# Unscaled attention maps, biases added on GpSimd, gate products as stages, and new order lists in a small vision tower with experts

## The chip, the cores and the metric

The kernel runs on one core of one Trainium2 chip, in float32 (a few counting matrices are bfloat16). The time is the device time of one execution in microseconds; the kernel before takes 390.56 us, the median of 3 runs (388.23 to 392.81).

## The reference

The input is 32 images of 3x96x96. Every image becomes 36 tokens of 128 features (1152 tokens in all), which pass through four blocks, each on the layer-normed sum so far, and each added to it. `norm` is a layer norm. Cut to what matters here:

```
h = tokens(x)                                  # patches, projection, norm
# block 1: attention with rotary positions, then a relu network; both normed behind the addition
src = norm(h)
x1 = norm(src + softmax(rope(q) rope(k)^T * hd**-0.5) v @ Wo.T, g1, be1)
h = h + norm(x1 + relu(x1 @ W1.T + b1) @ W2.T + b2, g2, be2)
# block 2: two lower-triangular products over the features
h = h + gelu(norm(h) @ tril(W1).T + b1) @ tril(W2).T + b2
# block 3: differential attention, then a group norm of the context
o = (softmax(q1 k1^T / sqrt(hd)) - lam * softmax(q2 k2^T / sqrt(hd))) v
h = h + (groupnorm(o) * gn_w + gn_b) @ out_w.T + out_b
# block 4: attention, then 64 experts, 2 for each token
x = norm(h); x = x + softmax(q k^T * hd**-0.5) v @ wo
x2 = norm(x); gates, ids = top_2(softmax(x2 @ wr))
y = gelu(x2[slots] @ w1[e] + b1[e]) @ w2[e] + b2[e]
h = h + x + sum over 2 of gate * y
```

There are 8 heads of 16 features, and an expert takes up to 72 tokens.

## The kernel before, in words

The tokens are worked on in four blocks of 8 images (288 tokens, `b` from 0 to 3). The way through the network is cut into stages, and a stage with its block is written `rope_scores:2`. The prefixes name the part: `tok` and `src` are the token stage and the first norm, `rope` is the attention of block 1, `x1`, `net` and `x2` its norm, network and second norm, `mix` block 2, `dif` and `gn` block 3, `moe` the attention of block 4, `rt` the routing. The endings name the work:

- `_norm_a`: VectorE takes the mean and variance (L1203, L1206), then GpSimd makes the reciprocal root in four small instructions (L611 to L615; more of them for `moe`). `_norm_b`: ScalarE applies it. `x2_norm_b` goes on: GpSimd multiplies and adds two rows (L663, L664), and VectorE adds it to `h` (L1327).
- `_turn`: TensorE transposes, and ScalarE copies back. `_qk`, `_v`: projections.
- `_scores`: TensorE makes the scores of all heads and pairs of images in four PSUM banks (`scores`), VectorE takes the row maximum (L1266) and subtracts it (L1275) into `ex`, ScalarE takes the exponential in place. A map is 100 partitions x 1152.
- `_sums`: VectorE sums the rows (L1284), takes the reciprocal (L1291) and multiplies the map by it (L1299) into `probs`. For `dif` the two maps are scaled in place, and `dif_mix` subtracts them (L1309) into `probs`.
- `_flip`: TensorE transposes the map in four parts (L803), ScalarE copies each into `pT`. `_pv`: TensorE multiplies by the values, and ScalarE copies the context to `ctxT`. `_out`: the output projection, which VectorE adds to the running sum (L1318).
- `mix_out` and `dif_out` open their bank with `biased`, a product of a row of ones and the bias row, so that the bias is in the sum.
- `gn_sum`, `gn_center`, `gn_var`, `gn_rstd`, `gn_apply`: the group norm. At its end VectorE multiplies by the scale, ScalarE adds `gn_b`, and only then `dif_out` can start.
- `rt_logits`, `rt_gate`, `rt_count`: VectorE finds the two best experts and their gates, TensorE counts the places, VectorE makes the slot numbers `flat_u`, and GpSimd sends the rows to their slots in DRAM with six indirect DMAs a block (L690). VectorE also makes `gm`, the gates as a matrix of tokens by experts, from which the bias of the experts' second layer comes.

What order the work has is written out by hand: `ORDERS_FOUND` has a list of stages for each of TensorE ("pe"), ScalarE ("act"), VectorE ("dve") and GpSimd ("pool"), and each engine works through its list strictly in order, waiting on semaphores. PSUM has four banks besides `scores`, and the jobs of TensorE go over them in rotation: `fill` waits until the reader of four jobs before is done. `AWAKE_FOUND` gives the number of filler products (`wT` by `wT`, 128x128) that TensorE does ahead of a stage, into the bank that the stage will use. A float32 product is two instructions in the trace, a transposition one.

Behind the lists, TensorE turns `gm`, multiplies by `b2` (`bias_turn`, `bias`), and VectorE copies (`bias_in`) and adds it to `h` (`bias_add`). Then for each of the six DMAs of the last block TensorE waits for its landing (`last_sent`) and does `PACE` fillers, then `HEAD_WARM` more. SyncE waits for the same landings and loads the rows of the experts in nine chunks of 2 to 8 experts (L570). TensorE transposes an expert's rows (L979), VectorE scales them (L1408), and the 64 experts run, one behind the other: 4 products of the first layer, gelu on ScalarE, 4 products of the second layer, VectorE scales by the gates (L1437), GpSimd scatters (L720). The weights come through a ring of 11. At the end the results are loaded, summed and stored.

What the change touches in the code: the lists and constants at the top, `taken`, `tokens`, `biased`, `flip`, `weigh`, the branches of `mix_out` and `dif_out`, `bias_turn` and `bias` on TensorE; `_scores` and `gn_apply` on ScalarE; `_scores`, `_sums`, `_out` and `bias_in` on VectorE.

## Time and profile before

| what | value |
| --- | --- |
| median of 3 runs | 390.56 us (388.23 to 392.81) |
| the profiled execution | 389.98 us |
| its span in the profile | 388.3 us |
| mean granted clock of TensorE | 0.959 |
| TensorE busy | 347.7 us (90%) |
| VectorE busy | 233.7 us (60%) |
| ScalarE busy | 220.9 us (57%) |
| GpSimd busy | 197.4 us (51%) |

The profile is of one execution. PE is TensorE, PEld its weight loads, DVE VectorE, ACT ScalarE, POOL GpSimd, SPq the queue of SyncE. Busy time is the time in which an engine had an instruction under way; TensorE's fillers count in it. The mean duration of TensorE's small products is longer than the time each adds, since they overlap. The granted clock is a share of 2.4 GHz: 1.00 is the upper level and 0.50 the lower (1.2 GHz). "Idle before" an instruction is given with what ended it.

### The profile page before, as it was taken

To read this page: it belongs to the slowest core of one execution; us is meant where nothing else is said; L and a number is where in the kernel's file an instruction comes from. 1 tells how busy PE (TensorE), PEld (TensorE's weight loads), DVE (VectorE), ACT (ScalarE), POOL (GpSimd) and SP (SyncE) were. 2 spreads that over 40 slices of the span, in tenths; PEclk is the share of its full clock that TensorE was granted. 3 is DMA by queue.
4 is the path that set the end of the run, shared out by engine and by line. 5 is a ranking of instruction groups with operands and counts; after the bars stand their busy time and mean duration, and the time that the engine had idled before them with its cause. 6 is when DMAs were issued, how large, how long until landed. Compare 5 with 4: busy or idle time off the path is not lost.

```text
span 388.3 us, 11371 instructions
## 1 busy us (share of the span) xinstructions
PE 347.7 (90%) x4424; PEld 315.2 (81%) x4424; DVE 233.7 (60%) x615; ACT 220.9 (57%) x640; POOL 197.4 (51%) x312
## 2 busy tenths in 40 slices
PE   8969799999988999997899899499999999999950
PEld 8748687887866889696778788399999999999950
DVE  1446788763489899897868985623335433333314
ACT  1247677777659876677488563103555555555520
POOL 3169687587841112236345767720555555555550
PEclk9999999999999999998999999559999999999995
DMA  7999924000000000000000100037899989999206
GB/s 277 374 391 334 150 28 125 2 2 1 2 3 0 3 3 2 3 2 3 3 3 2 33 9 13 15 95 202 272 320 316 322 308 316 327 324 314 85 9 182
DMA packets 21239, 50.20 MB, mean 129 GB/s; under 512 B 4116, under 2 KB 10340, under 8 KB 21058
## 3 DMA queue, kind: packets, MB, share of 16 engines
q1 hardware_dynamic: 18146, 46.96, 37.9%
q0 software_dynamic: 3040, 2.52, 2.4%
q8 instruction: 36, 0.59, 0.6%
q14 instruction: 17, 0.14, 0.1%
HBM read 43.97 MB, written 7.72 MB: 133 GB/s over the span
## 4 chain that ended last, share of the span: by engine, by line
PE 57%; DVE 12%; ACT 11%; POOL 9%; DMA 6%; issue 4%; SPq 1%; POOLq 0%; DVEq 0%
PE bank L728 34%; PE scores L728 18%; DMA lambdas<-in_lambdas 4%; ACT work L1037 4%; PE bank L803 3%; ACT norm L1037 3%; POOL rstd L613 3%; DVE mx L1266 2%; DVE stats L1203 2%; DVE work L1275 1%; ACT src L1037 1%; PE bank L979 1%; POOL rstd L611 1%; ACT xrow L1037 1%; POOL norm L664 1%
## 5 line engine op out<-in xcount | busy, mean ns | idle before, releaser
L1037 ACT ACTIVATE work<-scores,b1T 128x72 f32<-128x72 f32 x256 | 61.3, 322 | 66.9 <-PE scores L728 66.9
L728 PE MATMUL bank<-ring,work 128*72 128x128 f32 x512 | 97.3, 274 | 0.0
L720 POOL DMA_INDIRECT expert_rows<-work,put_u x64 | 59.9, 935 | 61.7 <-issue 37.7
L728 PE MATMUL scores<-work,ring 128*128 128x72 f32 x512 | 89.0, 258 | 0.2 <-ACT work L1037 0.2
L728 PEld LDWEIGHTS scores<-work,ring 128*128 128x128 f32 x512 | 76.9, 191 | 0.3 <-issue 0.3
L728 PE MATMUL bank<-wT 128*128 128x128 f32 x504 | 72.3, 283 | 2.7 <-ACT work L1037 2.7
L728 PEld LDWEIGHTS bank<-wT 128*128 128x128 f32 x504 | 63.8, 193 | 5.7 <-ACT work L1037 3.1
L1037 ACT ACTIVATE work<-bank 128x288 f32<-128x288 f32 (+3 forms) x136 | 46.7, 376 | 34.4 <-PE bank L728 27.0
L1437 DVE TENSOR_SCALAR work<-bank,work 72x128 f32<-72x128 f32 x64 | 22.2, 347 | 67.5 <-PE bank L728 67.5
L728 PEld LDWEIGHTS bank<-ring,work 128*72 128x72 f32 x512 | 53.8, 145 | 0.2 <-ACT work L1037 0.2
L611 POOL TENSOR_SCALAR rstd<-mv 96x3 f32<-96x3 f32 x32 | 10.1, 315 | 54.8 <-DVE mv L1206 53.6
L613 POOL TENSOR_TENSOR rstd<-rstd,minus_half 96x3 f32<-96x3 f32 x32 | 28.2, 882 | 2.7
L690 POOL DMA_INDIRECT slot_rows<-xrow,flat_u x24 | 24.0, 1001 | 10.5 <-issue 6.1
L1408 DVE TENSOR_SCALAR work<-bank,cols 128x72 f32<-128x72 f32 x64 | 21.7, 341 | 6.8 <-PE bank L979 6.8
L728 PE MATMUL bank<-xTp,wT 128*128 128x288 f32 x80 | 22.9, 416 | 2.3 <-ACT work L1037 1.4
L1037 ACT ACTIVATE work<-work 100x1152 f32<-100x1152 f32 (+1 forms) x20 | 20.2, 1016 | 8.3 <-DVE work L1275 7.0
L1266 DVE TENSOR_REDUCE mx<-scores 100x32 f32<-100x1152 f32 x16 | 21.6, 1351 | 5.0 <-PE scores L728 4.9
L728 PE MATMUL bank<-wT,xTp 128*128 128x128 f32 x192 | 23.8, 277 | 0.4 <-DVE work L1252 0.4
L728 PEld LDWEIGHTS bank<-wT,xTp 128*128 128x128 f32 x192 | 22.5, 192 | 1.4 <-issue 1.2
L1284 DVE TENSOR_REDUCE sm<-work 100x32 f32<-100x1152 f32 x16 | 21.4, 1340 | 3.5 <-ACT work L1037 3.3
L1299 DVE TENSOR_TENSOR work<-work,sm 100x1152 f32<-100x1152 f32 x16 | 21.8, 1360 | 0.6
L1275 DVE TENSOR_TENSOR work<-scores,mx 100x1152 f32<-100x1152 f32 x16 | 21.7, 1358 | 0.6
(159 smaller groups left out, 594.2 us busy)
## 6 DMA issues: line engine op xcount, KB each, us to landing
ring<-in_experts SPq DMA_DIRECT2D x64, 512.0 KB, 5.0
work<-in_patches SPq DMA_DIRECT2D x3, 864.0 KB, 10.6
slot_rows<-hid SPq DMA_DIRECT2D x1, 2340.0 KB, 30.2
work<-slot_rows SPq DMA_DIRECT2D x7, 292.5 KB
wT<-in_weights SPq DMA_DIRECT2D x1, 1664.0 KB, 13.9
expert_rows<-mid POOLq DMA_DIRECT2D x2, 576.0 KB, 5.1
ring<-expert_rows SPq DMA_DIRECT2D x4, 288.0 KB, 4.0
expert_rows<-work,put_u POOLq DMA_INDIRECT x64, 4.4
```

Source lines behind the costliest of these rows:

```text
L611: st.step(pool.tensor_scalar(n, m, -1.0, None, ALU.mult))
L613: st.link(pool.tensor_tensor(r, r, minus_half[0:TP, 0:TPB], ALU.pow))
L690: pool.indirect_dma_start(out=xslot[:, :], out_offset=bass.IndirectOffsetOnAxis(ap=flat_u[:, TPB * b + n, k:k + 1], axis=0), in_=xrow[:, b ...
L720: pool.indirect_dma_start(out=ytok[:, :], out_offset=bass.IndirectOffsetOnAxis(ap=put_u[:, e:e + 1], axis=0), in_=ys[0:CAP, e % NY, :], in ...
L728: return nc.tensor.matmul(o, a, b, start=start, stop=stop)
L1037: return nc.scalar.activation(o, i, f, **kw)
L1266: st.link(v.tensor_reduce(m3, sc, AX_X, ALU.max))
L1275: v.tensor_tensor(e4, sc, m3.unsqueeze(3).broadcast_to([SROWS, QUADS, 2 * PAIRS, SEQ]), ALU.subtract).then_inc(S["exp_in"], 1)
L1284: st.link(v.tensor_reduce(s3, e4, AX_X, ALU.add))
L1299: v.tensor_tensor(to, e4, s3.unsqueeze(3).broadcast_to([SROWS, QUADS, 2 * PAIRS, SEQ]), ALU.mult).then_inc(S["map_scaled" if stage[:3] == ...
L1408: v.tensor_scalar(xe[:, e % NX, :], banks[i][:, 0:CAP], col("L1_ffn_ln2_g"), col("L1_ffn_ln2_b"), ALU.mult, ALU.add).then_inc(S["xe_ready" ...
L1437: v.tensor_scalar(ys[0:CAP, f % NY, :], banks[f % 2][0:CAP, 0:D], xrows[0:CAP, f, D + 1:D + 2], None, ALU.mult).then_inc(S["ys_ready"], 1)
```

## The change

- In `rope` and `moe` the exponentials go from ScalarE straight to `probs`, unscaled, and `_flip` waits for the exponential alone. `_sums` only sums and takes the reciprocal, into `part_of_one`. A new stage `_flat` (TensorE, ScalarE) multiplies `part_of_one` by the identity, in four small products, so that the reciprocals lie as 8 heads by 288 tokens (`flat`). `_pv` has a second job: `spread` (which repeats a head's value over its 16 features) by `flat`. VectorE then multiplies `ctxT` by it (new stage in its list, L1362 of the new kernel), and `_out` waits for that.
- The bias rows of `mix_out` and `dif_out` are added by GpSimd (new stages `mix_norm_b`, `dif_norm_b`, L721 and the like of the new kernel, 96x384 each, 8 in all) into `mid`, and `_out` adds the product to `mid`; `biased` is gone. ScalarE's part of `gn_apply` is gone: `gn_b` is multiplied by the output weights once (new stage `fold`) and added to the row of `out_b`.
- `bias_turn`, `bias` and `bias_in` become stages `gate_turn` and `gate_bias` in the lists, with the copy on ScalarE and other banks.
- `HEAD_WARM` goes from 4 to 10, `PACE` from 3 to 4, and all the lists are new. The fillers of `AWAKE_FOUND` are 270 instead of 252; by part: tok 26 (16 before), src 10 (6), rope 12 (24), x1 3 (2), net 1 (4), mix 32 (38), dif 70 (64), gn 20 (14), moe 43 (39), rt 53 (45).

```diff
-HEAD_WARM = 4
-PACE = 3
+HEAD_WARM = 10
+PACE = 4
...
-    tok_z:0=5 tok_shift:0=4 tok_shift:1=1 tok_turn:1=2 tok_z:3=1 tok_turn:2=1 src_turn:0=3 rope_qk:0=4 tok_turn:3=2
+    tok_z:0=12 tok_shift:0=3 tok_shift:1=2 tok_z:2=2 tok_shift:2=2 tok_turn:2=4 src_turn:0=1 tok_turn:3=1
...
+                if stage == "mix_norm_b":
+
+                    pool.tensor_tensor(tiles(mid, b), tiles(h, b), row("L0_ffn_b2"), ALU.add).then_inc(S["mix_based"], 1)
+                if stage == "dif_norm_b":
+
+                    pool.wait_ge(S["folded"], 1)
+                    pool.tensor_tensor(tiles(mid, b), tiles(h, b), row("L1_attn_out_b"), ALU.add).then_inc(S["dif_based"], 1)
...
-            def biased(job, name):
-
-                o = fill(pe, job)
-                pe.wait_ge(S["rows_in"], 16)
-                mm(o[0:TP, 0:TPB * D], const("ones")[0:1, :], rows[0:1, ROWS.index(name), :].unsqueeze(1).broadcast_to([1, TPB, D]),
-                   start=True, stop=False)
...
-                    pe.wait_ge(S["probs_ready"], probs_count[name + "_sums", b])
+                    pe.wait_ge(S["exp_done"], soft_n[name + "_scores", b] + 1)
...
+                if name == "dif":
+                    return
+                job = (stage, b, 1)
+                o = fill(pe, job)
+                pe.wait_ge(S["flat_ready"], flat_count[name + "_flat", b])
+                mm(o[:, 0:TB], const("spread", H), flat[:, n % 2, :]).then_inc(filled(job), 1)
+
+            def flatten(stage, b):
+
+                job = (stage, b, 0)
+                o = fill(pe, job)
+                name = stage.split("_")[0]
+                pe.wait_ge(S["sums_ready"], soft_n[name + "_scores", b] + 1)
+                tokens_of = const("ident")[0:SROWS, :].rearrange("r (a k) -> r a k", k=HALF)[:, :, 0:SEQ]
+                for p in range(PAIRS):
+                    last = mm(o[0:H, 2 * SEQ * p:2 * SEQ * (p + 1)], part_of_one[:, flip_n[name + str(b)] % 2, p, :], tokens_of)
+                last.then_inc(filled(job), 1)
...
                 elif stage == "dif_out":
-                    biased((stage, b, 0), "L1_attn_out_b")
-                    pe.wait_ge(S["square_ready"], square_n["gn_apply", b])
-                    tokens((stage, b, 0), ctx_tile, [block_of("L1_attn_out_w")], open_=True)
+                    pe.wait_ge(S["gn_scaled"], b + 1)
+                    tokens((stage, b, 0), ctx_tile, [block_of("L1_attn_out_w")])
...
-            bias_turn(0)
-            bias_turn(1)
-            bias(0, banks[0])
-            bias_turn(2)
-            bias(1, banks[1])
-            bias_turn(3)
-            bias(2, scores[:, 2, :])
-            bias(3, scores[:, 3, :])
+            pe.wait_ge(S["gmT_ready"], NB)
...
+                elif stage in ("rope_pv", "moe_pv"):
+                    dve.wait_ge(S["ctx_ready"], ctx_count[stage, b])
+                    r = read(dve, (stage, b, 1))
+                    v.tensor_tensor(ctxT[:, tok], ctxT[:, tok], r[:, 0:TB], ALU.mult).then_inc(S["ctx_scaled"], 1)
...
-                    base = {"rope": src, "net": mid, "mix": h, "dif": h, "moe": src}[name]
+                    base = {"rope": src, "net": mid, "mix": mid, "dif": mid, "moe": src}[name]
+                    if stage in ("mix_out", "dif_out"):
+                        dve.wait_ge(S["mix_based" if stage == "mix_out" else "dif_based"], b + 1)
```

How the instructions now stand, at three places. The names are those of the tiles: `scores`, `bank` and `ex` (within `work`) as above, `sm` the row sums, `cst` the constants. First VectorE at the first attention map, before:

```order
L1266 TENSOR_REDUCE mx<-scores 100x32
L1275 TENSOR_TENSOR work<-scores,mx 100x1152
L1252 TENSOR_TENSOR work<-bank,cst 128x288 x4
L1284 TENSOR_REDUCE sm<-work 100x32
L1291 RECIPROCAL sm<-sm 100x32
L1299 TENSOR_TENSOR work<-work,sm 100x32x36
L1266 TENSOR_REDUCE mx<-scores 100x32
L1275 TENSOR_TENSOR work<-scores,mx 100x1152
```

And VectorE at the same place in the new kernel:

```order
L1298 TENSOR_TENSOR work<-bank,cst 128x288 x4
L1312 TENSOR_REDUCE mx<-scores 100x32
L1321 TENSOR_TENSOR work<-scores,mx 100x1152
L1386 TENSOR_TENSOR rows<-rows,bank 96x128
L1334 TENSOR_REDUCE sm<-work 100x32
L1335 RECIPROCAL part_of_one<-sm 100x4x4x2
L1312 TENSOR_REDUCE mx<-scores 100x32
L1321 TENSOR_TENSOR work<-scores,mx 100x1152
L1362 TENSOR_TENSOR work<-work,bank 128x288
```

The rotary products of the next block (x4) now stand ahead of the first map, the scaling of the map is gone, and a fold and the multiplication of the context have come in.

Second GpSimd between the first attention and the second norm, from `x1_affine:2` on, before:

```order
L714 TENSOR_TENSOR mid<-norm,rows 96x384
L715 TENSOR_TENSOR mid<-mid,rows 96x384
L611 TENSOR_SCALAR rstd<-mv 96x3
L612 TENSOR_SCALAR rstd<-mv 96x3
L613 TENSOR_TENSOR rstd<-rstd,minus_half 96x3
L615 TENSOR_TENSOR rstd<-rstd 96x3
```

And the same place in the new kernel:

```order
L733 TENSOR_TENSOR mid<-norm,rows 96x384
L734 TENSOR_TENSOR mid<-mid,rows 96x384
L721 TENSOR_TENSOR mid<-h,rows 96x384
L623 TENSOR_SCALAR rstd<-mv 96x3
L624 TENSOR_SCALAR rstd<-mv 96x3
L625 TENSOR_TENSOR rstd<-rstd,minus_half 96x3
L627 TENSOR_TENSOR rstd<-rstd 96x3
```

The new addition of a bias row, `mix_norm_b:0`, stands ahead of two reciprocal roots (one of them is listed).

Third TensorE at the end of the lists, from the last logits on, before (`wr` are the logits, `run` the last count, `wT` alone fillers, `gm` the gate turns and `b2nat` the gate products):

```order
L728 MATMUL bank<-wr,xT 96x64 x3
...
L728 MATMUL bank<-run,ones 96x64
L964 MATMUL scores<-cst,gm 64x96 x6
L728 MATMUL bank<-b2nat,work 96x128 x3
L964 MATMUL scores<-cst,gm 64x96 x3
L728 MATMUL bank<-b2nat,work 96x128 x3
L964 MATMUL scores<-cst,gm 64x96 x3
L728 MATMUL scores<-b2nat,work 96x128 x6
L728 MATMUL scores<-wT 128x128 x22
L979 MATMUL bank<-cst,work 128x72 x3
```

And in the new kernel:

```order
L747 MATMUL bank<-wr,xT 96x64 x3
L985 MATMUL scores<-cst,gm 64x96 x3
L747 MATMUL scores<-b2nat,work 96x128 x6
L747 MATMUL bank<-wT 128x128 x6
...
L747 MATMUL bank<-run,ones 96x64
L985 MATMUL scores<-cst,gm 64x96 x3
L747 MATMUL bank<-b2nat,work 96x128 x6
L747 MATMUL scores<-wT 128x128 x34
L1019 MATMUL bank<-cst,work 128x72 x3
```

Two of the four gate products and six fillers have moved ahead of the last count, only one gate turn and two products are left behind it, and 34 fillers stand where 22 stood.

## Rows read from the trace of the kernel before

**Rows 1.** Stretches: length, then busy us and instructions; PEclk, DMA share, GB/s.

```profile
38.20:85.10 46.90, 43.11 (x731) 37.51 (x730) 36.24 (x75) 33.72 (x86) 33.94 (x53) 1.00 0.40 65
85.10:110.10 25.00, 23.38 (x160) 19.04 (x158) 12.27 (x48) 16.95 (x40) 18.51 (x33) 1.00 0.00 1
110.10:187.00 76.90, 70.72 (x1277) 61.49 (x1277) 69.84 (x116) 56.08 (x127) 22.57 (x45) 0.98 0.01 2
187.00:235.50 48.50, 44.60 (x777) 39.63 (x776) 39.82 (x120) 33.52 (x87) 27.78 (x51) 1.00 0.04 11
235.50:248.40 12.90, 8.16 (x75) 7.23 (x73) 8.71 (x36) 4.08 (x8) 9.03 (x16) 0.83 0.05 13
248.40:256.70 8.30, 7.58 (x33) 6.03 (x33) 1.93 (x5) 0.00 (x0) 5.62 (x6) 0.50 0.05 12
256.70:264.60 7.90, 7.42 (x48) 7.22 (x47) 2.49 (x6) 0.00 (x0) 0.00 (x0) 0.73 0.65 173
264.60:374.40 109.80, 109.52 (x1086) 108.93 (x1086) 40.92 (x139) 61.33 (x256) 57.71 (x62) 1.00 0.80 271
```

**Rows 2.** Groups by line and form: busy us, mean ns of one, idle before.

```profile
L1284 DVE TENSOR_REDUCE sm<-work 100x32 f32<-100x1152 f32 x16 | 21.4, 1340 | 3.5 <-ACT work L1037 3.3
L1291 DVE RECIPROCAL sm<-sm 100x32 f32<-100x32 f32 x12 | 4.2, 353 | 0.4
L1299 DVE TENSOR_TENSOR work<-work,sm 100x1152 f32<-100x1152 f32 x16 | 21.8, 1360 | 0.6
L1252 DVE TENSOR_TENSOR work<-bank,cst 128x288 f32<-128x288 f32 x16 | 6.2, 448 | 0.0
L979 PE MATMUL bank<-cst,work 72*128 72x72 f32 x64 | 14.4, 228 | 0.5 <-DVE work L1408 0.5
L728 PE MATMUL bank<-xTp,wT 128*128 128x288 f32 x80 | 22.9, 416 | 2.3 <-ACT work L1037 1.4 <-DVE h L1318 0.9
L728 PE MATMUL bank<-rows,cst 1*96 1x384 f32 x16 | 7.0, 520 | 0.0
L1037 ACT ACTIVATE work<-work,cols 128x288 f32<-128x288 f32 x4 | 2.1, 526 | 0.0
```

**Rows 3.** Timeline (start, us), VectorE and GpSimd: an addition alone, and pairs that meet.

```profile
79.93 0.55 DVE L1327 TENSOR_TENSOR h<-h,norm 96x384 f32<-96x384 f32 x1 [0.28 <-POOL norm L664]
94.00 1.27 DVE L1327 TENSOR_TENSOR h<-h,norm 96x384 f32<-96x384 f32 x1 [2.81 <-POOL norm L664]
93.86 1.00 POOL L714 TENSOR_TENSOR mid<-norm,rows 96x384 f32<-96x384 f32 x1
54.27 1.36 DVE L1299 TENSOR_TENSOR work<-work,sm 100x1152 f32<-100x1152 f32 x1
54.30 1.37 POOL L615 TENSOR_TENSOR rstd<-rstd 96x3 f32<-96x3 f32 x1
```

**Rows 4.** Timeline of VectorE: the addition of the first attention's last block.

```profile
85.09 0.55 DVE L1318 TENSOR_TENSOR src<-bank,src 96x384 f32<-96x384 f32 x1 [1.72 <-PE bank L728]
```

**Rows 5.** Timeline: the last attention's last block on VectorE, and ten fillers on TensorE.

```profile
228.90 1.36 DVE L1299 TENSOR_TENSOR work<-work,sm 100x1152 f32<-100x1152 f32 x1
235.55 0.55 DVE L1318 TENSOR_TENSOR src<-bank,src 96x384 f32<-96x384 f32 x1 [0.92 <-PE bank L728]
224.56 2.48 PE L728 MATMUL bank<-wT 128*128 128x128 f32 x20
```

**Rows 6.** Timeline from the last scatters to the first expert, and GB/s of 256:266.

```profile
248.41 1.01 POOL L690 DMA_INDIRECT slot_rows<-xrow,flat_u  x1 [0.80 <-POOL xrow L681]
256.75 1.02 DVE L1399 TENSOR_TENSOR h<-bank,h 96x384 f32<-96x384 f32 x2 [2.20 <-DMA slot_rows<-xrow,flat_u]
256.79 7.16 PE L728 MATMUL scores<-wT 128*128 128x128 f32 x44
264.06 0.61 DVE L1408 TENSOR_SCALAR work<-bank,cols 128x72 f32<-128x72 f32 x2 [5.36 <-PE bank L979]
GB/s 65 7 0 0 0 0 4 83 254 83 87 262 287 316 241 229 200 200 200 200 166 200 200 200 200 200 200 200 200 200 200 200 200 200 200 200 200 200 200 200
```

261 lines of the change are left out of this document (150 added, 111 removed).

## The prediction

> **What bounds the kernel now.** I first cut the run into stretches [rows 1]. From 264.6 to 374.4 us TensorE is busy for 109.52 of 109.80 us at granted clock 1.00 (the upper of its two levels, 2.4 GHz): the 64 experts. The change leaves their instructions alone, so this stretch and the 13.9 us behind it only shift. Ahead of it stand 264.6 us. TensorE is busy there too, but with filler multiplications in part, which the list of fillers adds to keep its clock up, so its share says little. The engine to look at is VectorE: 36.24 of 46.90 us in the first attention, 12.27 of 25.00 in the stretch behind it, 69.84 of 76.90 in the differential one, 39.82 of 48.50 in the last one. So VectorE sets the pace in the attentions, nearly without gaps in the differential one. In 85.1 to 110.1 it idles for half the time: there GpSimd is busy for 18.51 of 25.00 us with reciprocal roots and affine steps.
>
> Then I read the groups of costs [rows 2]: each attention map costs VectorE a sum (1340 ns), a reciprocal (353) and a scaling multiplication (1360). Last I read the way from the last attention block to the first expert [rows 6]: the final scatter lands at about 256.75 (VectorE waited for it 2.20 us), TensorE starts 22 fillers (x44, two instructions each) at 256.79 and needs 7.16 us, and VectorE then reads the first turned expert input at 264.06. The nine loads of rows are issued from 256.8 on. In the window 256 to 266, cut in 40 parts of 0.25 us, traffic starts at 257.5. By 258.5 about 106 KB have moved (4, 83, 254 and 83 GB/s, times 0.25 us), and the first load has 73 KB. So the fillers, not the load, end this wait.
>
> **The first attention, 38.2 to 110.1.** The scaling goes: 4 x 1.36 = 5.44 us of VectorE. In its place comes a multiplication of the context, 128x288 with one operand in PSUM. Its nearest row is the 128x288 multiplication from PSUM at 448 ns [rows 2]: 4 x 0.45 = 1.8. The fold (96x128, once) has no row; it lies between a few tenths and the 0.55 us that the 96x384 addition takes [rows 5], I take 0.3. VectorE saves 5.44 - 1.8 - 0.3 = 3.3 us.
> The map may also be turned as soon as the exponential is there; sum, reciprocal and scaling (3.05 us) no longer stand ahead of it. At 85.09 VectorE had waited 1.72 us for the last block's product [rows 4]; of such waits I take back 1.5.
> Against it, GpSimd gets eight additions of 96x384 at 1.0 us ([rows 3], L714). One stands ahead of the x2 roots, where GpSimd is the engine waited for: +1.05. The second must be done before the mix_out:1 addition of VectorE, which stood right behind x2_norm_b:3; behind that wait in VectorE's queue are the norms and the first differential maximum: +0.45. TensorE gets, per attention block, 4 small products and one of 128x288. By the nearest rows (228 ns for one instruction of 72x72, 416 for one of 128x288, which overlap) that is at least 0.7 and at most 4 x 2 x 0.23 + 2 x 0.42 = 2.7 us; I take 1.0, since its instructions overlap like the 288-wide ones (22.9 us for 80). Fillers in the rope stages fall from 24 to 12, and at 0.248 us each (2.48 us for 10, [rows 5]) 3.0 us of them make room for 4.0. Net I book nothing there. If that cover is gone the cost is the product's whole 4 x 2.7 = 10.8 us less 3.0.
> Sum: -3.3 - 1.5 + 1.5 = -3.3 us. Ends: +4 (no wait returns, each extra step on the way) and -7.
> The start is booked at nothing: seven more fillers stand before tok_z:0 (1.7 us), but later patches were waited for anyway, and rope_qk:1 is only moved ahead of the first maximum.
>
> **The differential attention, 110.1 to 187.** VectorE's work stays. Gone are ScalarE's shift by gn_b (526 ns, four times, on the way to dif_out) and the bias products (7.0 us for 16 instructions, [rows 2]) from mix_out and dif_out. Since VectorE idles for only 7.06 us here, that is all there can be to win; I take 1. New are the other six or seven GpSimd additions, where GpSimd is busy for 22.57 of 76.90 us. They are free by occupancy, but they share something with VectorE [rows 3]: the same VectorE addition h+norm takes 0.55 us alone and 1.27 us when GpSimd's L714 has started 0.14 us before it, and GpSimd's little L615 takes 1.37 us instead of 0.19 when it starts 0.03 us behind VectorE's scaling. Each addition can hold up VectorE by 0 to 1.0 us. VectorE's operations with both operands in SBUF (8 scalings of 1.36 us, 4 differences of the same shape, 8 of 128x288 at about 0.45) fill some 20 of the 77 us, so roughly one addition in three meets one, for half its length: I take +1. Sum 0, ends -5 and +5.
>
> **The last attention and the routing, 187 to 256.7.** VectorE saves 4 x (1.36 - 0.45) = 3.6 us. Of the last block, 6.65 us passed from the start of the scaling (228.90) to the addition of its product (235.55) [rows 5]. Now, from the end of the reciprocal, VectorE does the routing of block 2 (about 3.1 us, as before), the context multiplication 0.45, then waits for the product, about 1.5: 5.1, so -1.5. Ahead of the last turn, logits and count stand eight more fillers net (2.0 us), mostly beside waits: +0.6. Behind it the chain is kept: roots, norm, count, six scatters of about 1.27 us from 248.41 on. Sum -4.5, ends -8 and 0.
>
> **The bias products and the wait for the first expert.** The gate turns and products become stages before the scatters land, and 24 of the 34 fillers are spread over the six waits for scatters. Behind the last one remain 4 + 10 = 14. At 0.248 us they take 3.5 us, where 7.16 stood; at half clock 14 x 0.43 = 6.0 (7.16 us for 22 already mixes both levels). The load has landed by then. The row of 248.4 to 256.7 shows 0.50 granted, though TensorE was busy for 7.58 of 8.30 us, so I take a little off the 3.7: -3.3, ends -1.1 and -4. If they lagged more, the load (2 us) would not be what is late next but the fillers again.
>
> **The sum.** -3.3 + 0 - 4.5 - 3.3 = -11.1 us against the profiled run's 389.98 us (span 388.3 and 1.68 around it): 378.9. The median of the runs is 390.56, 0.6 above the profiled one, so 379.5.
>
> **Rivals.**
> 1. GpSimd's queue takes the gain. For: its additions (8.4 us) and the excluded pairs above; and the first six scatters (7.6 us) stand ahead of rt_norm_a:2 in its queue, while VectorE's list now has the statistics of that step sooner behind them; in TensorE's queue the turn of that block stands ahead of the last map's turning. Price: the first attention's 3.3 us vanish and about 1.5 in the last: 384.3. Against: GpSimd idles for over two thirds of the differential stretch.
> 2. More comes back: VectorE's idle time in the differential and last attention (7.1 + 8.7 us) shrinks by a third, since the maps turn earlier and the banks come free sooner: -5, so 374.5. Against: those waits are for work that mostly stays.
> 3. Slower: TensorE's clock falls in the first attention. The place is 38.2 to 85.1, where it was at 1.00 with 43.11 of 46.90 us busy, and where half of the fillers go. Only the stretch behind 248.4 shows the lower level (0.50, 1.2 GHz), after one in which TensorE was busy for 8.16 of 12.90 us [rows 1]. At half clock some 38 us of real work (43.11 less about 5 of fillers) become 76. Over half of the stretch that adds some 15 us against the 11 gained: 395. It decides from about a third of the stretch at half clock. Against: 4 us of new products per attention fill the same places.
> 4. The lists keep their old waits and only the end gains: 390.6 - 3.3 = 387.3, with small costs 388.5.
>
> **How the numbers follow.** The forecast gets 0.50, rival 1 0.20, rival 2 0.16, rival 3 0.08, rival 4 0.06. A measurement here tells about 1% (3.9 us) from no change. Faster by more than that (under 386.7): forecast and rival 2 nearly whole, most of rival 1: 0.82. Within 1%: rival 4, the rest of rival 1 and little of rival 3: 0.10. Slower: 0.08. The range goes from 373 (rival 2) to 388 (rival 1 and part of rival 4).
>
> **What would show it.** Right: the scaling rows at half their count (8 of 16), eight context multiplications near 0.45 us; the differential stretch still about 77 us long with VectorE over 90% busy; 3 to 4 us from the last landed scatter to the first turned input plus 0.3; the expert stretch again 110 us. Wrong: TensorE's clock under 0.9 before the routing; VectorE's two-input rows well over 1.36 us; GpSimd as releaser of VectorE or ScalarE for longer in sum than before; an end wait that is still over 6 us.

## The result, and the profile after

The changed kernel takes **392.09 us** (389.04 to 394.71, 20 runs), the kernel before 390.65 us (388.23 to 393.46, 20 runs): a ratio of 1.0047, 95% interval [1.0028, 1.0067]. It is slower by half a per cent, within the 1% that I called no change. Forecast were 379.5 us and a range of 373 to 388. The profiled execution took 391.9 us, its span is 390.2.

To see where the forecast 11 us went I put the same events of the two traces side by side, start to start:

| event | before | after | difference | added in this part |
| --- | --- | --- | --- | --- |
| first map maximum | 38.24 | 40.52 | +2.3 | +2.3 |
| last context addition of the first attention | 85.09 | 94.49 | +9.4 | +7.1 |
| first differential maximum | 111.09 | 119.17 | +8.1 | -1.3 |
| first maximum of the last attention | 179.07 | 186.24 | +7.2 | -0.9 |
| last landed scatter | 256.75 | 260.80 | +4.1 | -3.1 |
| first scaled expert input | 264.06 | 265.74 | +1.7 | -2.4 |
| span | 388.3 | 390.2 | +1.9 | +0.2 |

From the differential attention on it goes much as forecast. All of the loss lies ahead of the last context addition at 94.49 us, so I looked there first. In the slices of the span (40 of 9.76 us each) the fifth and sixth stand out, TensorE's busy share in the one and its clock in the other (the last line is the clock of the kernel before, in its slices of 9.71 us):

```profile
PE   8999699999999899999999999799999999999950
...
PEclk9999969999999999999999999969999999999995
...
PEclk9999999999999999998999999559999999999995
```

The granted clock fell in the sixth slice, where the kernel before kept it at 8 or 9 up to the routing. The stretches of 2 us show what came ahead of that fall (columns as in [rows 1]):

```profile
46.00:48.00 2.00, 0.00 (x0) 0.00 (x0) 0.53 (x2) 0.45 (x2) 1.39 (x2) 0.99 1.21 163
48.00:50.00 2.00, 0.96 (x25) 0.77 (x26) 0.19 (x1) 0.00 (x0) 0.59 (x1) 0.50 0.88 110
50.00:52.00 2.00, 2.00 (x13) 2.00 (x13) 1.97 (x2) 0.57 (x2) 0.00 (x0) 0.50 0.20 36
52.00:54.00 2.00, 2.00 (x14) 1.78 (x13) 0.56 (x1) 1.07 (x3) 0.00 (x0) 0.50 0.00 0
54.00:56.00 2.00, 2.00 (x73) 1.57 (x70) 0.00 (x0) 1.01 (x3) 0.00 (x0) 0.81 0.00 0
```

TensorE did nothing at all in 46 to 48 us, and from 48 on its clock was at 0.50 (1.2 GHz) for about 7 us, of which it idled for the first one. The timeline of TensorE tells what it had been doing, the 64 products of one map:

```profile
44.42 0.69 PE L747 MATMUL scores<-work 32*36 32x72 f32 x40
49.04 0.71 PE L747 MATMUL scores<-work 32*36 32x72 f32 x24 [3.93 <-issue]
```

It stopped in the middle of `rope_scores:1`, and the wait has no releaser: "issue" means that nothing the profile shows was waited for. No semaphore stands between those products. The trace of before has the same stop, half as long, and its clock stayed at 1.00:

```profile
44.45 0.78 PE L728 MATMUL scores<-work 32*36 32x72 f32 x52
47.05 0.35 PE L728 MATMUL scores<-work 32*36 32x72 f32 x12 [1.82 <-issue]
```

Up to the stop, both traces have 341 matrix instructions of TensorE. The same count in two programs with other work ahead of it points to the instructions themselves: their next block was not there. The DMA queues have rows for such blocks. In the kernel after one of 16 KB (0.02 MB in the row) lands in 46 to 47 us:

```profile
q1 hardware_dynamic: 294, 0.15, 117.2%
q8 instruction: 1, 0.02, 8.7%
```

The columns are packets, MB and the time they took as a share of the 16 engines. In the kernel before the corresponding block stands in 43 to 44. So the packet's row doesn't stand at the end of the stop but some 3 us ahead of it, in both kernels. This distance keeps in all that follows, as I read it in windows of 0.1 us:

| kernel | instructions done | block's packet | stop ends |
| --- | --- | --- | --- |
| before | 341 | 43.9 | 47.05 |
| after | 341 | 46.1 | 49.04 |
| run 3 | 341 | 46.8 | 49.69 |
| run 4 | 341 | 46.4 | 49.43 |
| run 10 | 341 | 43.0 | 45.70 |
| run 1 | 341 | 41.1 | no stop; the next instruction at about 45.5 |
| run 3 | 842 | 80.0 | 82.25 |
| run 12 | 842 | 73.2 | 76.01 |
| run 14, again | 842 | 73.4 | 75.89 |
| after | 842 | 75.4 | no stop; the next instruction at about 80.0 |

A stop ends 2.2 to 3.2 us behind its packet; where the packet is over 4 us ahead of the instruction, none shows.

In both kernels, the ordinary queue q1 beside it is full (over 100% of the engines): it still carries the eleven expert loads and, last, the zeroing of the slot rows, 2.3 MB in packets of some 520 bytes, at about 150 GB/s.

VectorE's waits ahead of its context multiplications, the first three blocks' in turn:

```profile
56.14 0.45 DVE L1362 TENSOR_TENSOR work<-work,bank 128x288 f32<-128x288 f32 x1 [3.58 <-PE bank L747]
66.54 0.46 DVE L1362 TENSOR_TENSOR work<-work,bank 128x288 f32<-128x288 f32 x1 [4.38 <-PE bank L747]
81.14 0.45 DVE L1362 TENSOR_TENSOR work<-work,bank 128x288 f32<-128x288 f32 x1 [3.13 <-PE bank L747]
```

The stretches of after, which answer to [rows 1], and the groups that answer to [rows 2]:

```profile
40.50:93.00 52.50, 46.77 (x749) 40.05 (x750) 30.60 (x70) 32.77 (x82) 31.17 (x55) 0.93 0.30 51
116.30:187.00 70.70, 66.97 (x1212) 59.70 (x1210) 66.83 (x116) 52.69 (x122) 27.14 (x49) 1.00 0.01 3
248.40:256.70 8.30, 5.78 (x38) 5.14 (x39) 3.80 (x13) 1.69 (x2) 5.95 (x8) 0.76 0.06 15
256.70:264.60 7.90, 7.90 (x61) 7.90 (x60) 1.95 (x4) 0.00 (x0) 2.31 (x3) 0.82 0.30 83
```

```profile
L1347 DVE TENSOR_TENSOR work<-work,sm 100x1152 f32<-100x1152 f32 x8 | 10.9, 1358 | 0.3
L1362 DVE TENSOR_TENSOR work<-work,bank 128x288 f32<-128x288 f32 x8 | 3.6, 454 | 15.6 <-PE bank L747 14.1 <-ACT work L1070 1.6
L747 PE MATMUL bank<-cst,part_of_one 100*8 100x72 f32 x64 | 5.8, 238 | 0.5 <-ACT work L1070 0.5
L747 PE MATMUL bank<-flat,cst 8*128 8x288 f32 x16 | 5.9, 450 | 0.0
L725 POOL TENSOR_TENSOR mid<-h,rows 96x384 f32<-96x384 f32 x4 | 4.1, 1045 | 0.0
```

VectorE's busy time in the first attention fell from 36.24 of 46.90 us to 30.60 of 52.50. Of these 5.6 us, 1.5 are the four rotary products that now stand ahead of the stretch, and a context multiplication of 0.45 falls just behind it; the rest fits the 3.3 us that were to be saved. But the eight context multiplications, 3.6 us of work, have 15.6 us of waiting ahead of them, 12.5 in the first attention. The new products cost TensorE 5.8 + 5.9 = 11.7 us over eight blocks, 1.46 each.

The end is read from VectorE's last rows ahead of the experts [rows 6]:

```profile
260.80 1.02 DVE L1453 TENSOR_TENSOR h<-scores,h 96x384 f32<-96x384 f32 x2 [8.12 <-DMA slot_rows<-xrow,flat_u]
...
265.74 0.61 DVE L1462 TENSOR_SCALAR work<-bank,cols 128x72 f32<-128x72 f32 x2 [3.00 <-PE bank L1019]
```

4.94 us from the landing to the first input, where 7.31 stood. The fillers had been meant to spread over the waits for the scatters. They did not:

```profile
252.79 0.66 PE L985 MATMUL scores<-cst,gm 96*64 96x96 f32 x3 [2.52 <-issue]
253.38 2.87 PE L747 MATMUL bank<-b2nat,work 64*96 64x128 f32 x12
256.18 9.46 PE L747 MATMUL scores<-wT 128*128 128x128 f32 x68
...
252.33 0.35 DVE L1447 TENSOR_TENSOR gm<-oh 96x192 f32<-96x192 f32 x1
```

All 34 (x68) ran without a gap from 256.18 on. Ahead of them TensorE idled for 2.52 us. This wait has no releaser in the profile either, but it is of another kind than the one at 341. It stands between two groups and ahead of the last gate turn, which waits for `gm`, and VectorE's row for `gm` ends at 252.68, just before. It is 2.5 us long in every changed kernel (but the disturbed one of run 14), at counts from 3359 to 3401, so it goes with the event. Behind it came the gate products at half clock, 2.87 us, and only then the fillers.

### The profile page after: what moved, and what is told of

Its sections match the earlier page's. It is cut to its first block, busy times and chain, and to the rows that moved or that the text cites. A ratio compares the mean times of both kernels' runs of the same rounds, so it can differ in the third digit from the quotient of the medians.

```text
span 390.2 us, 11671 instructions
## 1 busy us (share of the span) xinstructions
PE 357.5 (92%) x4550; PEld 327.0 (84%) x4550; DVE 226.6 (58%) x612; ACT 222.2 (57%) x648; POOL 201.2 (52%) x320
## 3 DMA queue, kind: packets, MB, share of 16 engines
q0 software_dynamic: 3040, 2.52, 2.4%
## 4 chain that ended last, share of the span: by engine, by line
PE 65%; ACT 14%; POOL 7%; DVE 7%; issue 4%; DMA 1%; POOLq 0%; DVEq 0%; SPq 0%
PE bank L747 41%; PE scores L747 18%; ACT work L1070 6%; PE bank L814 4%; ACT norm L1070 2%; POOL rstd L625 2%; ACT hid L1070 1%; PE bank L1019 1%; PE bank L756 1%; DVE stats L1249 1%; ACT L1070 1%; ACT src L1070 1%; DMA ring<-expert_rows 1%; ACT h L1070 1%; DVE mx L1312 1%
## 5 line engine op out<-in xcount | busy, mean ns | idle before, releaser
L747 PE MATMUL bank<-wT 128*128 128x128 f32 x540 | 78.3, 285 | 0.0
L747 PEld LDWEIGHTS bank<-wT 128*128 128x128 f32 x540 | 68.6, 195 | 4.4 <-issue 1.3
L1070 ACT ACTIVATE work<-bank 128x288 f32<-128x288 f32 (+3 forms) x136 | 46.8, 376 | 39.5 <-PE bank L747 24.8
L623 POOL TENSOR_SCALAR rstd<-mv 96x3 f32<-96x3 f32 x32 | 8.6, 268 | 42.6 <-DVE mv L1252 41.2
L702 POOL DMA_INDIRECT slot_rows<-xrow,flat_u x24 | 22.6, 942 | 11.1 <-issue 6.1
L814 PE MATMUL bank<-cst,work 100*128 100x100 f32 x192 | 21.0, 263 | 1.5 <-ACT work L1070 0.9
L1321 DVE TENSOR_TENSOR work<-scores,mx 100x1152 f32<-100x1152 f32 x16 | 21.7, 1358 | 0.5
L814 PEld LDWEIGHTS bank<-cst,work 100*128 100x128 f32 x192 | 18.7, 148 | 3.5 <-ACT work L1070 2.9
```

The lines of the kernel that those rows point to most:

```text
L623: st.step(pool.tensor_scalar(n, m, -1.0, None, ALU.mult))
L702: pool.indirect_dma_start(out=xslot[:, :], out_offset=bass.IndirectOffsetOnAxis(ap=flat_u[:, TPB * b + n, k:k + 1], axis=0), in_=xrow[:, b ...
L747: return nc.tensor.matmul(o, a, b, start=start, stop=stop)
L814: last = nc.tensor.transpose(o[:, SROWS * q:SROWS * (q + 1)], probs[0:SROWS, n % 2, q, p, :, :].rearrange("p a k -> p (a k)"), const("iden ...
L1070: return nc.scalar.activation(o, i, f, **kw)
L1321: v.tensor_tensor(e4, sc, m3.unsqueeze(3).broadcast_to([SROWS, QUADS, 2 * PAIRS, SEQ]), ALU.subtract).then_inc(S["exp_in"], 1)
```

## The experiments

Fourteen kernels ran, one of them twice. Each ratio is to the kernel before as it ran in the same group of runs. Three causes stood against each other for the loss in the first attention: (A) the stop for instructions and the clock behind it, (B) VectorE's waiting in the order of its list for the relay of reciprocals over TensorE, (C) the new order of the start.

**1 and 2. No backlog when the block is due.** In both kernels the zeroing goes out behind the small loads, and each ring load waits for one more map:

```diff
-            for e in range(RING):
-                sp.dma_start(ring[:, e, :], ins["experts"][e]).then_inc(w_here[e], 16)
             sp.wait_ge(S["blank_made"], 1)
             sp.dma_start(xslot.rearrange("(p n) c -> p n c", p=D), ...)
+            for e in range(RING):
+                sp.wait_ge(S["s_full"], 3 + e)
+                sp.dma_start(ring[:, e, :], ins["experts"][e]).then_inc(w_here[e], 16)
```

> The changed kernel with its early DMA traffic moved out of the first attention: the zeroing of slot_rows goes straight behind the small loads, and each of the 11 expert weight loads of the ring waits for a later map of scores (the 3rd to the 13th). Theory A (TensorE's instruction block is fetched late behind the DMA backlog, TensorE stops in its 342nd product, its clock falls, and VectorE's list waits in order behind it): the stop of 3.9 us at 45 us shrinks below 0.5, the granted clock stays at 1.00 up to 93 us, the first differential maximum comes 6 to 9 us earlier than 119.2, and the time falls to 382 to 386. Theory B (the relay over flat, spread and the context multiplication makes VectorE wait whatever TensorE does): the stop goes but VectorE still waits over 10 us for L1362's bank, and the time falls by less than 4, to 388 or more.

> The kernel before with the same move of the DMA traffic. Theory A: it has the same stop at the same product (341 products done) but only of 1.8 us and no fall of the clock, so it gains 1 to 2.5 us, to about 388.5 to 389.5, and the changed kernel comes out ahead of it by 4 us or more. Theory B: it gains the same 1 to 2.5 us, and the changed kernel stays within 2 us of it.

Measured: the changed kernel with this edit **384.3 us** (383.05 to 385.64), ratio to before 0.9839 [0.9778, 0.9900]. The kernel before with it 390.74 us, ratio 1.0016 [0.9978, 1.0054]. The map products of the changed one run in one piece, and its first attention is at 1.00 throughout:

```profile
45.17 0.89 PE L748 MATMUL scores<-work 32*36 32x72 f32 x64
```

So the edit gives the changed kernel 7.8 us, and the kernel before nothing, where I had expected 1 to 2.5. There too the stop is gone (its second maximum stands at 44.61 instead of 47.47), but by the first differential maximum only 0.9 of 2.9 us are left: ScalarE had to wait 5.12 us for GpSimd's roots, where it had waited 3.53. Without the stop the change is worth 384.3 - 390.7 = -6.4 us.

Not all of the 7.8 us is the stop's. By the trace 6.0 lie ahead of the first differential maximum (113.17 against 119.17), and 1.4 in the end wait (3.58 us against 4.94). The end wait has these two lengths in other kernels too: 3.6 in runs 6 and 12, 5.0 in runs 7 and 10, where no stop at 341 is longer than 0.35. They go with how long the clock stays at 0.50 behind the wait for `gm`, some 3.4 us in run 1, 6.8 in the kernel after and 6.7 in run 10. Why it differs isn't shown.

Those two stop-free traces are the right pair to price the terms of the forecast with: first maximum +3.8 (41.26 against 37.47), from there to the first differential maximum -0.8, so +3.0 up to it; differential attention -0.7 (67.07 against 67.81); last attention and routing -3.4; end wait -3.6 (3.58 against 7.22). Each is one trace. The first maxima of runs 5, 8 and 9, whose start is the same, stand at 41.54, 40.61 and 40.80, so the +3.8 and the +3.0 are known to within about 1 us.

**3. Fewer fillers ahead of `tok_z:0`** (5 instead of 12, all else as changed).

> The changed kernel with 5 fillers instead of 12 ahead of tok_z:0, as before the change. Theory A: what decides is which product is the 342nd and when its block is fetched. With 7 products fewer ahead, the stop falls 7 products later in the same scores (it stays in rope_scores:1 or just behind it), the fetch is asked for at about the same time, and the time stays within 1.5 us of 392.1. If instead the 1.7 us of extra fillers at the start were what is lost, the first maximum (40.52) comes over 1 us earlier and the whole gets 1.5 us faster.

Measured 395.41 us (393.94 to 395.96), ratio 1.0113 [1.0054, 1.0173], outside the 1.5 us that I had allowed. The 7 fillers are 14 instructions. The stop moved by exactly so many, from behind the 40th map product instruction to behind the 54th, and stood again at a count of 341. It is bound to a place in the stream of instructions, not to an event:

```profile
49.69 0.48 PE L747 MATMUL scores<-work 32*36 32x72 f32 x10 [4.45 <-issue]
82.25 0.28 PE L747 MATMUL bank<-work 128*32 128x36 f32 x9 [1.67 <-issue]
178.44 2.27 PE L747 MATMUL bank<-wT 128*128 128x128 f32 x18 [1.40 <-issue]
```

Two further stops appeared, which the kernel after doesn't have, and each cost about what it lasted: the events behind the first (at a count of 842) came 1.9 us later, those behind the second another 1.4. The first maximum stood where it had (40.53), so those fillers cost nothing at the start, as booked.

**4. Few fillers in the wait for the scatters** (`HEAD_WARM = 4`, `PACE = 1`).

> The changed kernel with PACE 1 and HEAD_WARM 4: 10 fillers instead of 34 between the gate products and the first expert. If the fillers still end the wait (as the trace says: 9.46 us of them in one piece, the last 4.6 behind the last landing), the first scaled input comes 2 to 2.5 us earlier behind the last landing, when the load has landed. If the clock is then low at the first experts, up to 2 us of it are given back. Time 389.7 to 391.5.

Measured 395.03 us (393.86 to 397.57), ratio 1.0113 [1.0071, 1.0155], where I had expected a small gain. The end wait fell from 4.94 to 2.68 us, but from the first input to the first sum that the list `SUM_AT` puts between the experts (L1483) it took 32.0 us instead of 27.6, at a lower clock. The fillers between the landings buy more than they cost.

**5. VectorE's list: the next maximum ahead of the context multiplication.** This run and runs 6 to 9 stand on the kernel of 384.3 us.

```diff
-    ... rope_sums:1 rope_pv:1 rope_out:1 x1_norm_a:1 rope_scores:2 rope_qk:3
+    ... rope_sums:1 rope_scores:2 rope_pv:1 rope_out:1 x1_norm_a:1 rope_qk:3
-    ... x2_norm_a:0 rope_pv:2 rope_scores:3 rope_out:2
+    ... x2_norm_a:0 rope_scores:3 rope_pv:2 rope_out:2
```

> The changed kernel with its early transfers held back (384.3 us), and in VectorE's list the maximum and difference of block 2 put ahead of the context multiplication of block 1, those of block 3 ahead of that of block 2. There VectorE waited 4.39 and 3.17 us in list order, with a ready map behind the wait. If what remains of the loss in the first attention is this waiting in order (theory: the context multiplication sits in VectorE's list ahead of work that is ready), the first differential maximum comes 3 to 5 us sooner and the time is about 380. If the waits only stand where TensorE's or GpSimd's own chain is late (rival), they move elsewhere and the time stays within 1 us of 384.3.

Measured 385.37 us (384.58 to 386.48), ratio 0.9898 [0.9812, 0.9984]. The two waits are gone and the third maximum runs 6 us earlier:

```profile
58.09 1.36 DVE L1313 TENSOR_REDUCE mx<-scores 100x32 f32<-100x1152 f32 x1 [1.71 <-PE scores L748]
...
60.78 0.46 DVE L1363 TENSOR_TENSOR work<-work,bank 128x288 f32<-128x288 f32 x1
```

The first differential maximum stood at 113.38 instead of 113.17: nothing gained. Cause B falls, as far as it is the order of VectorE's list. The 7.5 us of waiting that went were idle time of an engine that isn't the bound there. What the relay itself adds on TensorE and ScalarE no run takes away.

**6 and 7. The order of the start as before.** First the order of the four lists alone, then with before's fillers at those stages (10 more):

```diff
-    tok_shift:3 src_turn:0 rope_v:0 rope_qk:0 src_turn:1 tok_turn:3 rope_qk:1 fold:0 rope_scores:0 rope_v:1
+    tok_shift:3 src_turn:0 rope_qk:0 tok_turn:3 rope_v:0 rope_scores:0 src_turn:1 rope_qk:1 fold:0 rope_v:1
```

> The same base (384.3 us), with the start in the order of the kernel before on all four engines: query and key products of block 0 ahead of the values, the second block's rotation behind the first maximum. If the 2.3 to 3.8 us by which the first maximum is late (38.24 and 37.47 in the two kernels before, 40.52 and 41.26 in the changed ones) comes from that order, the first maximum falls to about 38.5 and the time to about 382. If the start is hidden behind later waits, as the prediction booked it (nothing), the time stays within 1 us of 384.3.

> As the run with the start in the order of before (388.6 us, where the clock fell to 0.50 in 32 to 38 us), and with the fillers of before at the five stages of the start. If the fall came from the 10 fillers that were missing there, the clock stays at 1.00, and the time is that of the order alone: 382 to 384. If the order itself costs, it stays near 388.

Measured 388.62 us (385.42 to 389.63), ratio 0.9950 [0.9906, 0.9995], then 388.37 us (387.04 to 389.01), ratio 0.9951 [0.9918, 0.9984]. In the first the clock fell, with no stop for instructions near it. The stretches of that run:

```profile
30.00:34.00 4.00, 2.65 (x10) 1.61 (x9) 3.41 (x12) 1.92 (x6) 3.35 (x10) 0.75 1.23 152
34.00:38.00 4.00, 4.00 (x18) 3.72 (x17) 1.52 (x5) 2.23 (x6) 2.78 (x4) 0.50 0.41 54
```

TensorE had been busy for 2.65 of 4 us, and went on at half clock. With the 10 fillers the clock stayed at 1.00 and the first maximum came at 38.84 instead of 41.26; yet the first context addition came at 55.65 instead of 52.88, and the first differential maximum 2.7 us later. (The other 1.4 us of what the run lost are the end wait of 5.0.) Cause C falls too: the late first maximum is paid back by what the new order has ready sooner.

**8. Fewer fillers at the end, at the same pace** (`HEAD_WARM` 4 instead of 10).

> The same base (384.3 us), with 4 fillers behind the last landed scatter's own 4 instead of 10. Theory that only their number counts: 6 x 0.25 = 1.5 us less, 382.8. Theory that the clock in the first experts needs them: the wait shrinks by 1.5 and the experts take it back, 384 or more; with one filler per scatter and 4 behind them the experts took 4.4 us longer.

Measured 383.76 us (383.29 to 385.50), ratio 0.9845 [0.9763, 0.9927]: not told apart from 384.3. Its end wait is 3.65 us, no shorter: the clock was low again behind the gate products, and its 28 fillers took 9.09 us, where 34 had taken 9.46.

**9. GpSimd's additions cut to 4 of 128 columns.**

```diff
-pool.tensor_tensor(tiles(mid, b), tiles(h, b), row("L0_ffn_b2"), ALU.add)
+pool.tensor_tensor(tiles(mid, b)[:, :, 0:4], tiles(h, b)[:, :, 0:4], row("L0_ffn_b2")[:, :, 0:4], ALU.add)
```

The additions of the other row are cut in the same way. The kernel leaves out most of the two bias rows; waits and order stay.

> The same base (384.3 us), with GpSimd's eight bias additions cut to 4 of their 128 columns (it leaves most of the two bias rows out; waits and order stay). The prediction priced these additions at +1.5 us ahead of the differential attention and +1 in it: by that the time falls by 2.5 to 381.8. If they lie beside other work (rival), it falls by less than 1. By the port rival alone (every addition meets a two-input operation of VectorE) it would fall by 5 or more.

Measured 382.74 us (382.34 to 383.93), ratio 0.9830 [0.9745, 0.9914]: 1.6 less than with them, which the runs alone hardly tell apart. The trace does. By it, 0.6 us of it lie between the first maximum and the first differential one (71.32 against 71.91), 0.8 in the differential attention (66.26 against 67.07).

**10. The zeroing first, and nothing held back.** Which of the two parts of the backlog holds up the block?

> The changed kernel (392.1 us), in which only the zeroing of the slot rows is sent ahead of the eleven expert loads, which wait for nothing. The instruction block is due at about 45 us. If any full queue holds it up (the expert loads too, which then run until about 50), the stop in the map products of block 1 stays at 2 us or more and the time at 388 to 393. If only the zeroing's many small packets hold it up, which then are over by about 36, the stop is under 1 us and the time as with both held back, 384 to 385.

Measured **386.04 us** (384.45 to 386.58), ratio 0.9877 [0.9820, 0.9934]. The stop shrank to 0.35 us, although the expert loads had the queues full. The stretch beside the stop, in this kernel:

```profile
44.00:46.00 2.00, 1.65 (x72) 1.34 (x70) 0.94 (x1) 1.98 (x5) 1.85 (x7) 1.00 1.02 410
```

```profile
45.70 0.46 PE L747 MATMUL scores<-work 32*36 32x72 f32 x24 [0.35 <-issue]
```

At 410 GB/s in large packets the block came nearly in time; at 150 GB/s in small ones it was 2 to 4 us late. So it is the long line of small packets, not full queues as such. A single move of two lines gives this. The first differential maximum stands at 113.14, as with everything held back (113.17); the 1.7 us between the two kernels lie in the end wait (4.99 against 3.58), which the order of the loads isn't shown to change.

**11. Start as before, its fillers, and 4 at the end.**

> The best candidates together: early transfers held back, order and fillers of before at the start, 4 fillers instead of 10 behind the last landing. The latter alone gave 383.8 against 384.3, which is within what is measured. If the start gives 1 to 2 us, 382 to 383; if not, 384.

Measured 387.26 us (386.42 to 390.71), ratio 0.9954 [0.9914, 0.9994]: the start's loss again.

**12 to 14. TensorE's own queue.** The 10 fillers between 46 and 63 us go (2.5 us): on the kernel of 384.3, then with the list of 5 and the end of 8 besides, then on the kernel of 386.0.

```diff
-    ... src_turn:2=7 rope_flip:0=1 rope_flat:0=1 rope_flip:1=1 src_turn:3=1 rope_pv:1=2 x1_turn:0=2 rope_out:1=3
+    ... src_turn:2=7 src_turn:3=1
```

> The changed kernel with its early transfers held back (384.3 us), without the 10 fillers (20 instructions, 2.5 us) at six stages of the first attention between 46 and 63 us. Theory that TensorE's own queue bounds this stretch, so that VectorE's saved 4 us became idle time: the last context addition of the first attention and the first differential maximum come 1.5 to 2.5 us sooner, the time is about 382.5. Theory that TensorE waits there for others anyway: under 0.5 us. Rival with the clock: it falls to half in that stretch, as it did where 10 fillers were missing at the start, and the time rises to 387 or more.

> The same without the 10 fillers, with the two maxima put ahead of the context multiplications in VectorE's list, and with 4 fillers instead of 10 behind the last landing. Alone the order gave nothing (385.4) and the 4 fillers little (383.8). If VectorE's order matters once TensorE's queue is shorter, 381; if not, as the run without the fillers, 382 to 383.

> The changed kernel with the zeroing sent ahead of the expert loads (386.0 us), without the 10 fillers between 46 and 63 us. No load is on the queues behind 54 us, so no fetch of instructions meets one. If TensorE's queue bounds the first attention, the first differential maximum comes 1 to 2.5 us sooner than 113.1 and the time is 384 to 385. If TensorE waits there for others anyway, 386. If too few fillers drop the clock there even without a stop for instructions, it comes later than 113.1 and the time is over 387.

> The same kernel as the run before it, in which the kernel before took 398 us. In the trace of that run the clock fell to 0.50 in 76 to 80 us without a stop ahead of it, and the first differential maximum stood at 116.4 instead of 113.1. If the fall comes from the missing fillers, it is there again and the time is 388 to 390. If it was part of the disturbance, the clock stays at 1.00 and the time is 384 to 386.

Measured 387.51 us (386.31 to 388.29), 388.28 us (385.97 to 391.52), and for the last 408.4 us in a group of runs in which the kernel before took 398.1 (ratio 1.0271 [1.0202, 1.0340]). Its trace has further waits of 0.4 to 1.1 us in 218 to 248 us which no other has, so I set its time aside; run again, 388.71 us (387.65 to 391.03), ratio 0.9991 [0.9953, 1.0029]. None gained, and runs 12 and 14 met what their expectations had named as the sign of a fallen clock. From the first to the third maximum the first gained 1.0 us (21.97 against 22.94) and the last 1.2. Then came a stop, in the one with no load on the queues too (which has another of 0.86 us at 466). TensorE's timeline in the last one:

```profile
72.25 0.67 PE L747 MATMUL bank<-cst,part_of_one 100*8 100x72 f32 x8 [1.64 <-ACT work L1070]
72.85 0.89 PE L747 MATMUL scores<-work 32*36 32x72 f32 x64
73.67 0.74 PE L747 MATMUL bank<-work 128*32 128x36 f32 x61
75.89 0.26 PE L747 MATMUL bank<-work 128*32 128x36 f32 x3 [1.49 <-issue]
76.08 0.75 PE L747 MATMUL bank<-flat,cst 8*128 8x288 f32 x2
```

and its stretches, with the lower clock behind them:

```profile
72.00:76.00 4.00, 2.26 (x136) 1.92 (x136) 0.00 (x0) 1.35 (x5) 2.80 (x4) 1.00 0.02 4
76.00:80.00 4.00, 4.00 (x27) 3.57 (x26) 3.04 (x3) 3.10 (x9) 0.92 (x1) 0.77 0.02 4
```

The stop stands at a count of 842 here, as in runs 3, 12 and 13 (0.58 us). The clock, though, doesn't hang on this stop alone. In run 13 it was at 0.53 in 72 to 74 us, ahead of the stop, behind a stretch of 2 us with 0.56 busy; in the first run of the last kernel it fell at about 75 us with no stop at 842 at all. And in run 3 it stayed at 1.00 behind a stop of 1.67 us.

The kernels with all fillers pass that count without a stop. Their instruction block landed in 69 to 70 us; without the fillers none landed there, but one in 73 to 74. I read this so: the block is called for when TensorE reaches a certain instruction, without the fillers that comes later against the work, behind a wait for ScalarE, and then 125 short matrix instructions follow in 1.6 us and run out of instructions. That a late call is the cause is my inference from where the packets land; no run tried it alone. The Trainium skill (Runtime: NRT & Kernel Launch, "Instruction fetch mechanics") says that an engine's instructions are fetched in blocks of 16 KB over a DMA queue of its own while the one before runs, and that crossing a block's end is mostly hidden. The blocks and their queue are in these traces; hidden they weren't, with stops of 1.4 to 4.5 us in the rows above.

## Why the prediction was wrong

Forecast were -11.1 us, measured +1.4 in the medians and +1.9 in the spans. Of the 13 us between, 11.4 lie ahead of the first differential maximum. Two steps failed there. A bound was read from a busy share, and the clock and TensorE's flow of work were taken as given, though a stop in the trace of before spoke against it.

**The bound.** "VectorE sets the pace in the attentions" was read from its busy share (36.24 of 46.90 us), and this step failed for the first attention. Run 5 took 7.5 us of its waits for the context products away (9.1 to 1.6) and moved nothing. The chain of waits (the work that ended last, followed back) tells the same, cut to 41 to 113 us, of the two stop-free kernels, before and after:

```profile
by line: PE bank L729 22.7%; POOL rstd L614 9.9%; issue 9.3%; ACT norm L1038 6.8%; PE bank L804 5.4%; ACT work L1038 4.5%; POOL norm L665 4.4%; POOL norm L664 4.1%; DVE stats L1204 2.9%; POOL rstd L612 2.9%; POOL mid L716 2.8%; POOL rstd L6
```

```profile
by line: PE bank L748 32.9%; ACT work L1071 8.4%; ACT hid L1071 5.9%; PE bank L815 5.0%; issue 4.8%; DVE stats L1250 3.8%; PE scores L748 3.7%; POOL rstd L626 3.7%; ACT norm L1071 3.2%; POOL norm L677 3.0%; POOL norm L676 2.7%; ACT xT L1071
```

These are shares by line. Added up by engine, of some 72 us, the chain of the kernel before has GpSimd 24, TensorE 23, ScalarE 10, VectorE 9: VectorE is 13% of it, and busy beside it for the rest. In the changed kernel TensorE has 31, ScalarE 16, GpSimd 14, VectorE 8. So what GpSimd's part lost, TensorE's and ScalarE's took over; TensorE's products into the banks alone take 32.9% instead of 22.7%, 7 us more.

**The start and the first attention, forecast 0 and -3.3.** Measured without the stop +3.8 and -0.8, together +3.0 (runs 1 and 2); with it +2.3 and +5.8, together +8.1. The start, booked at nothing, was not nothing; run 7 shows that it can't be priced alone, since the order of before brings the first maximum back and loses more behind it. The other terms: VectorE's 3.3 us were saved and became idle time. The late waits, 1.5 to be taken back, grew instead. TensorE's new products were booked at 1.0 us a block and at nothing net; they measured 1.46, and TensorE was busy for 24.27 us between the second and the last context addition, where 20.63 stood. This is nearest to the end of +4 that I gave the term. GpSimd's +1.5 measured 0.6. How much of the +3.0 is due to the products, how much to the length of the relay and how much to the order of the new lists stays open: taking fillers away, which should have shown it, ran into another stop and a lower clock.

**The clock, rival 3 with 0.08.** Its place (the first attention, half of the fillers gone) was right, and a clock at half did turn the gain into a loss. Its trigger was another: a stop of 3.93 us for instructions, of which the trace of before showed 1.82 us, as a row with "issue" in the very stretch that I had read. I hadn't asked what it was. From the stop come 2.1 us more than before, and from the half clock about 2.9 by my estimate (5.7 us of work between 49.04 and about 54.8); this fits the 5.1 by which +8.1 exceeds +3.0. Run 6, run 13 and the first run of 14 show that the rival's own trigger exists too: 10 fillers fewer, and the clock fell with no stop for instructions ahead of it.

**The differential attention, forecast 0.** Measured -0.9. Of its two parts, GpSimd's +1 measured 0.8 (run 9). GpSimd's additions stopped VectorE where they met, as in the rows below, 1.19 us for an operation of 0.46. That was rare: the eight scalings and four differences of maps in the stretch kept their 1358 and 1354 ns in the mean.

```profile
158.44 2.16 POOL L725 TENSOR_TENSOR mid<-h,rows 96x384 f32<-96x384 f32 x2
158.56 1.19 DVE L1408 TENSOR_TENSOR work<-work,gn_s 128x288 f32<-128x288 f32 x1
```

**The last attention and the routing, forecast -4.5.** Measured -3.1, and -3.4 without the stop: right in kind, a quarter short.

**The end wait, forecast -3.3.** Measured -2.4 in the kernel after and -3.6 in the stop-free one, where 3.58 us are left, the 3.5 of 14 fillers. The term had 24 of the 34 fillers done in the waits for the scatters. TensorE came to the first of them only at 256.18, behind its wait for `gm` and the gate products, 4.6 us ahead of the last landing. So they ran until about 265.5, 4.7 us behind it. The term took a little off for lagging fillers, but not this.

**Rival 1** (GpSimd's queue takes the gain) had the time of run 1 within 0.1 us (384.3) by luck, since its mechanism isn't what the runs show: the trace of run 9 gives all of the eight additions 1.4 us. **Rival 4** (only the end gains) was nearer on the first attention than the forecast and wrong on the last. **Rival 3**, at 395, is the nearest to what was measured, by its time too.

Of the sum, -11.1, the terms behind 110 us forecast -7.8 and measured -7.7 (stop-free) and -6.4 (as it is). That these meet so well is in part luck, as the end wait alone differs by 1.4 from kernel to kernel. The prediction failed in one stretch, by one misread bound and one unread row. The best kernels found are the changed one with its early transfers held back, 1.6% faster than before, and the same with fewer fillers at the end (run 8), not told apart from it; with the zeroing merely sent first it is 1.2% faster.

## What to carry to other kernels

A wait with no releaser in the middle of a run of like instructions, at the same instruction count in several traces, was a wait for instructions here: look for it on the busiest engine before a change, since a small edit moves its place and its length. One between two groups, whose count changes from kernel to kernel, was a plain wait for another engine whose releaser the profile left out. Send long lines of small packets (zeroing, scatters of narrow rows) before the large loads, so that they are over when the dense part of the program begins. And before work is taken off an engine, look whether the chain of waits passes over it: here a busy share of 77% stood beside 13% of the chain, and the saving turned into idle time.

## What the runs showed of the hardware

- TensorE stopped for 1.8 to 4.5 us at a block of its instructions (16 KB) when the queues held a line of packets of some 520 bytes (140 to 165 GB/s), for 0.35 us when they held large loads at 410 GB/s, and not at all when they held nothing (runs 1 and 2).
- The block's packet stood 2.2 to 3.2 us ahead of the end of the stop, in all eight stops of the table.
- Stops of 1.82 (before) and 1.67 us (run 3) left the granted clock at 1.00; behind one of 3.93 (after) it was at 0.50 for about 7 us. Behind 72 to 76 us of run 14, with 2.26 us busy in them and a stop of 1.49 that followed a wait of 1.64, it was at 0.77 in the next 4. So the length of one stop doesn't tell what the clock does.
- Behind 125 short matrix instructions in 1.6 us TensorE stopped for 1.49 us with next to nothing on the DMA queues (4 GB/s).
